# Moving the expert and combine stages of a fused conv, attention and expert kernel in its schedule

## The reference

```python
x = x + conv3x3(group_norm(x, 32 groups), W0)            # 64 -> 64 channels, pad 1
t = tokens(x)                                            # (8, 3136, 64)
a = layer_norm(t)
q, k, v = a @ Wq.T + bq, a @ Wk.T + bk, a @ Wv.T + bv
t = t + softmax(q @ k.T / 8) @ v                         # over all 3136 tokens of an image
y = layer_norm(t)
gates = top 2 of softmax(y @ gate_w + gate_b), normalised to sum 1     # 16 experts
t = t + sum over the 2 experts e of gate_e * ((silu(y @ w1[e]) * (y @ w2[e])) @ w3[e])
```

## Time and profile before

| | |
|---|---|
| median of 3 runs | 3304.51 us |
| profiled execution | 3304.37 us, its span 3301.5 us |
| PE busy | 2755.8 us (83%) |
| DVE, ACT, POOL busy | 1950.5, 1426.9, 1004.9 us |
| granted PE clock | 0.92 of full speed on average |
| last score matmul of the attention | starts at 2899.9 us |
| last slice of the experts copied | 3194.6 us |

### The profile page before, as it was taken

How to read it: one execution, slowest core, us unless ns; L and a number is a source line. 1 busy time by engine, 2 the same in 40 slices (tenths; PEclk the granted TensorE clock), 3 DMA queues, 4 the chain that set the end, 5 groups by cost and what they waited for, 6 DMA issues and landing times.

```text
span 3301.5 us, 47374 instructions
## 1 busy us (share of the span) xinstructions
PE 2755.8 (83%) x14345; PEld 1688.3 (51%) x14345; DVE 1950.5 (59%) x5316; ACT 1426.9 (43%) x3169; POOL 1004.9 (30%) x1084
## 2 busy tenths in 40 slices
PE   0489998998999999998999899998999898967760
PEld 0245554554555555555555455554555555545550
DVE  1366667667666666668566765667656656442221
ACT  0134444444555544554445454454544454523330
POOL 4000002221212134234242332423324323347444
PEclk9679999999999999999999999999999999965555
DMA  6200000111111111211112111111111111123321
GB/s 142 63 21 20 19 16 26 30 29 33 47 43 41 44 44 50 54 44 52 51 50 52 49 49 51 50 49 40 50 47 41 38 43 43 42 64 91 82 60 31
DMA packets 218415, 156.13 MB, mean 47 GB/s; under 512 B 94400, under 2 KB 208832, under 8 KB 218176
## 3 DMA queue, kind: packets, MB, share of 16 engines
q1 hardware_dynamic: 187008, 106.12, 12.2%
q0 software_dynamic: 31168, 46.98, 5.9%
HBM read 89.29 MB, written 63.70 MB: 46 GB/s over the span
## 4 chain that ended last, share of the span: by engine, by line
PE 58%; DVE 24%; issue 8%; POOL 6%; ACT 2%; DMA 2%; SPq 1%; POOLq 0%; DVEq 0%; ACTq 0%
PE ps_o L1060 17%; DVE max_part L788 9%; PE ps_s L1047 8%; PE ps_m L1026 8%; PE ps_s L1049 6%; PE ps_x L1202 5%; PE ps_z L1085 4%; POOL got L515 3%; PE ps_x L1217 2%; PE ps_z L1210 1%; POOL sorted_x L502 1%; PE ps_y L1136 1%; PE ps_y L1120 1%; DVE top_i L845 1%; DVE got L944 1%
## 5 line engine op out<-in xcount | busy, mean ns | idle before, releaser
L788 DVE TENSOR_REDUCE max_part<-ps_m 112x1 f32<-112x448 f32 x1568 | 947.9, 621 | 528.5 <-PE ps_m L1026 518.9
L636 ACT ACTIVATE prob<-ps_s 112x448 f32<-112x448 f32 x1568 | 848.9, 543 | 598.8 <-PE ps_s L1049 575.1
L1026 PE MATMUL ps_m<-k_a,q_a 128*112 128x448 f32 x1568 | 589.3, 394 | 140.4 <-DVE max_part L788 129.5
L1060 PE MATMUL ps_o<-prob,v_s 112*64 112x448 f32 x3136 | 695.9, 566 | 0.3 <-issue 0.3
L1047 PE MATMUL ps_s<-q_a,k_a 128*112 128x448 f32 x1568 | 661.9, 422 | 16.0 <-ACT prob L636 9.9
L1049 PE MATMUL ps_s<-q_b,k_a 128*112 128x448 f32 x1568 | 573.5, 366 | 0.0
L502 POOL DMA_INDIRECT sorted_x<-xn,slot x448 | 427.3, 954 | 283.7 <-issue 260.3
L515 POOL DMA_INDIRECT got<-sorted_y,slot x448 | 424.9, 948 | 213.8 <-issue 126.5
L1026 PEld LDWEIGHTS ps_m<-k_a,q_a 128*112 128x112 f32 x1568 | 276.4, 176 | 311.1 <-DVE max_part L788 273.1
L525 POOL TENSOR_TENSOR ln_s<-ln_s,minus_half 112x4 f32<-112x4 f32 x56 | 58.1, 1037 | 1175.7 <-DVE ln_s L706 1175.7
L1047 PEld LDWEIGHTS ps_s<-q_a,k_a 128*112 128x112 f32 x1568 | 276.2, 176 | 184.5 <-issue 123.4
(11 more groups left out here) (170 smaller groups left out, 3004.0 us busy)
## 6 DMA issues: line engine op xcount, KB each, us to landing
fx<-sorted_x SPq DMA_DIRECT2D x48, 384.0 KB
sorted_y<-fy SPq DMA_DIRECT2D x48, 320.0 KB, 3.1
fx<-sorted_x SPq DMA_DIRECT2D x56, 256.0 KB
xh<-in_x SPq DMA_DIRECT2D x96, 126.0 KB, 2.7
x_st<-in_x SPq DMA_DIRECT2D x100, 112.0 KB, 2.6
sorted_x<-fy POOLq DMA_DIRECT2D x24, 320.0 KB
sorted_x<-xn,slot POOLq DMA_INDIRECT x448
got<-sorted_y,slot POOLq DMA_INDIRECT x448
```

Source lines behind the costliest of these rows:

```text
L636: a.activation(prob[(at.n * TILES + i) % PROBS][:], ps_s[i % 2][0:TILE, 0:CHUNK], ACT.Exp).then_inc(s["p_ready"], 1)
L788: v.tensor_reduce(max_part[:, m % PER, m // PER:m // PER + 1], ps_m[m % 2][0:TILE, 0:CHUNK], AX.X, ALU.max).then_inc(s["max_red"], 1)
L1026: t.matmul(ps_m[m % 2][0:TILE, 0:CHUNK], q_a[:, bass.ds(n % 2, 1), j * TILE:(j + 1) * TILE].rearrange("p a c -> p (a c)"), k_a[u % 2][:, k ...
L1060: t.matmul(ps_o[side:side + CHANNELS, 0:CHUNK], v_s[u % 2][:, i, :], prob[(n * TILES + i) % PROBS][:], start=(i < 2), stop=(i >= TILES - 2 ...
```

## The change

- **Experts** follow 11 bodies behind the attention instead of 15 (`LAG["experts"] = CHUNKS + 4`). Their slices of an image then fall on the bodies with c = 4, 5, 6, 0, 1, 2, 3, and no longer on c = 1 to 6 and 0. The short slice of 2 pairs was in c = 0 beside the routing; it is now in c = 3.
- **Scatter**: the seven scatters of an image, one in each body before, are done in three bodies: one at the end of c = 0 (after the routing), three in c = 1, three in c = 2. In c = 1 and c = 2 the first of them is ahead of norm2 and norm1, the rest behind norm1. In bodies 57 and 58, where there is no attention, all three are first. Consecutive scatters count on two semaphores.
- **Combine**: images 0 to 5 are combined in four bodies: two chunks in c = 5, two in c = 6, two in c = 0, one in c = 1. Of two chunks in a body the first has DVE at step 11, PE and ACT at step 12; the second has steps 19 and 21, as before. Images 6 and 7 are combined in bodies 61 to 74, one in each, at steps 22 and 23. Gather buffers and `tc` are doubled: a gather waits for the combine before the last, and it is issued in the body before its combine.
- **Experts without attention**: body by body, all pairs go through one pipeline that doesn't stop at body ends: at step 1 + 4 * place PE has fx of pair k, hidden of k-1, down of k-3, turn of k-2. "hidden" alternates between the two score banks `ps_s`. `fy` is doubled. SP stores a slice one body later, behind the loads of the slice after next and behind the body's output store.

```diff
-LAG = {"pre": -CHUNKS, "post": 1, "scatter": 1 + CHUNKS, "experts": 1 + 2 * CHUNKS, "combine": 1 + 3 * CHUNKS}
+LAG = {"pre": -CHUNKS, "post": 1, "experts": CHUNKS + 4}
+SCATTERS = ((0,), (1, 2, 3), (4, 5, 6), (), (), (), ())
+COMBINES = {5: (0, 1), 6: (2, 3), 7: (4, 5), 8: (6,)}
+COMBINE_AT, COMBINED_AT = (11, 19, 22), (12, 21, 23)
+LATE = ALL + 5
+LAST = LATE + 2 * CHUNKS - 1
...
+    def combines(self):
+        if self.n >= LATE:
+            return [(2, ALL - 2 * CHUNKS + self.n - LATE)] if self.n <= LAST else []
+        image, place = (self.u - 3, self.c + CHUNKS) if self.c < 2 else (self.u - 2, self.c)
+        chunks = COMBINES[place] if place in COMBINES and 0 <= image < BATCHES - 2 else ()
+        return [(slot + 2 - len(chunks), CHUNKS * image + c) for slot, c in enumerate(chunks)]
+
+    def stores(self):
+        if self.attends:
+            return [self] if self.active("experts") else []
+        ends = self.n == ALL + LAG["experts"] - 1
+        return [At(*divmod(n, CHUNKS)) for n in range(self.n - 1, self.n + ends) if ALL <= n < ALL + LAG["experts"]]
...
+def expert_steps(at):
+    if at.attends:
+        return [(i, name, at, pair) for i, _, name, pair in EXPERT_STEPS
+                if at.active("experts") and pair < at.pair_count()]
+    steps, pairs = [], alone_pairs()
+    here = [k for k, (mine, _) in enumerate(pairs) if mine.n == at.n]
+    if here and here[-1] == len(pairs) - 1:
+        here += [len(pairs) + k for k in range(3)]
+    for place, k in enumerate(here):
+        for name, behind in (("fx", 0), ("hidden", 1), ("gated", 1), ("down", 3), ("turn", 2)):
+            if 0 <= k - behind < len(pairs):
+                steps.append((1 + 4 * place, name) + pairs[k - behind])
+    return steps
...
             def body(at):        # SP
-                if at.active("combine"):
-                    k = at.index("combine")
-                    wait_apart(sp, s["c_ready"], ONE + k)
+                for _, k in at.combines():
+                    if k >= 1:
+                        wait_apart(sp, s["c_ready"], ONE + k - 1)
...
                 load_slice(at, 0)
-                if at.active("combine") and at.attends:
-                    store_out(at)
+                for place, k in at.combines():
+                    if place == 0:
+                        store_out(k)
                 load_slice(at, 1)
-                if at.active("combine") and not at.attends:
-                    store_out(at)
+                for place, k in at.combines():
+                    if place:
+                        store_out(k)
...
-            def gather(at):
+            def gather(k):
...
-                wait_apart(pool, s["c_ready"], ONE + k)
+                if k >= 1:
+                    wait_apart(pool, s["c_ready"], ONE + k - 1)
...
             def body(at):        # POOL
-                for stage, name in (("scatter", scatter), ("post", norm2), ("pre", norm1), ("combine", gather)):
-                    if at.active(stage):
-                        name(at)
+                early = at.scatters() if at.c else []
+                early = early[:1] if at.attends else early
+                for m in early:
+                    scatter(m)
+                if at.active("post"):
+                    norm2(at)
+                if at.active("pre"):
+                    norm1(at)
+                for _, k in At(*divmod(at.n + 1, CHUNKS)).combines():
+                    gather(k)
+                for m in at.scatters()[len(early):]:
+                    scatter(m)
...
             def body(at):        # PE; ACT and DVE alike
+                    for place, k in at.combines():
+                        if i == COMBINED_AT[place]:
+                            combined(k)
+                    for step, name, mine, pair in experts:
+                        if step == i:
+                            expert(mine, name, pair)
```

More of the change, by code:

```diff
@@ L106, in index @@
     def index(self, stage):
[L108 to L114, removed]
+        return min(max(self.n - LAG[stage], 0), ALL)
     def active(self, stage):
@@ L418, in _ @@
[L418 to L427, removed]
-                body(five, (u + 1, CHUNKS - 1))
-                body(At(u, CHUNKS - 1), (u + 2, 0) if u + 2 < BATCHES else None)
+                for place, k in at.combines():
+                    if place:
+                        store_out(k)
@@ L430, in _ @@
+            for n in range(-CHUNKS - 1, LAST + 1):
+                at, nxt = [At(*divmod(m, CHUNKS)) for m in (n, n + 1)]
+                body(at, (nxt.u + 1, nxt.c) if n >= -CHUNKS and nxt.u + 1 < BATCHES else None)
             sp.wait_ge(s["stored"], ONE + 16 * ALL)
@@ L499, in scatter @@
                     wait_apart(pool, s["fx_b_in"], ONE + (b - 1) * (CHUNKS - 1) * 16)
-                for j in range(at.chunk("scatter") * PER, (at.chunk("scatter") + 1) * PER):
+                for j in range(c * PER, (c + 1) * PER):
                     for k in range(TOP):
@@ L644, in body @@
                             events[name](at)
-                    for step, _, name, pair in (EXPERT_STEPS if at.attends else EXPERT_STEPS_ALONE):
-                        if step == i and at.active("experts") and pair < at.pair_count():
-                            expert(at, name, pair)
+                    for place, k in at.combines():
[4 more added lines that the diff above has]
+                            expert(mine, name, pair)
                     if i == NEXT_QUERIES and at.ahead:
@@ L968, in body @@
                             events[name](at)
-                    for step, _, name, pair in (EXPERT_STEPS if at.attends else EXPERT_STEPS_ALONE):
-                        if step == i and at.active("experts") and pair < at.pair_count():
-                            expert(at, name, pair)
+                    for place, k in at.combines():
+                        if i == COMBINE_AT[place]:
+                            combine(k)
+                    for step, name, mine, pair in experts:
+                        if step == i:
+                            expert(mine, name, pair)
                     if i == 3 and at.u == -1:
@@ L1195, in expert @@
                             for j in range(2 * (last - first)):
[L1196 removed]
+                                picked[2 * (f - pair + first) + j] = (code >> (j * DIGIT)) & (EXPERTS - 1)
                 elif name == "hidden":
[L1198 removed]
+                    (bank_x if at.attends else bank_h[f % 2]).take(("hid_ready", f + 1))
                     pe.wait_ge(s["fxT_ready"], ONE + f + 1)
```

179 lines of the change are left out of this document (91 added, 88 removed).

## The result

The changed kernel takes 3299.3 us (median of 17 runs, 3295.9 to 3304.0), the kernel before 3304.5 (17 runs, 3299.9 to 3310.1): ratio 0.9984, interval 0.9977 to 0.9991. That is 5 us faster where 13.5 were forecast. Its profiled span is 3295.9 us.

A forecast was written before the change was run, and what follows sets the result against it. PE bounds 56 bodies, then latencies and POOL's DMAs set a 401.6 us tail. Terms: -103 + 26.5 - 5 + 62 + 6 = -13.5, from 3304.4 to 3291 us; own range 3275 to 3306, 8 in 10 3243 to 3327.

The forecast's parts named there:

- part 3: Combines under the attention: 17 early ones at 4.9 us each, 83 + 40 - 61 = +62 us.
- rival A: Early combines under attention cost 7 us each, the clock down behind the wait: 36 us more, 3327; chance 0.20.
- The group norm's power behind a gather: POOL's order in c = 6: the power comes some 1.6 us late, DVE and PE wait, 4 bodies, +6 us.
- Routing beside pairs: Routing bodies get 3 more pairs, c = 3 loses 3; PE's idle time swallows part: -5 us for 6 bodies.
- 26.5: Under the attention: 17 more pairs at 1.56 us each, +26.5 us.
- The late combine's 1.8: In attention bodies, a combine at steps 19 and 21 costs 1.8 us.
- the pair's 1.56: In attention bodies, an expert pair costs 1.56 us beside the attention.
- The tail: From the last scores to the span's end: 299 us against 401.6, a loss of 103 us.
- Rival B: Early combines under attention cost no more than late ones: 53 us less, 3238; chance 0.15.
- C: Tail: the pipeline keeps PE full at the upper clock, a place at 1.9 us, total 3273; chance 0.18.
- D: c = 0 and 1: late slots put norm2 behind two scatters, 3 us in 7 bodies, 21 in all, 3312; chance 0.05.
- E: Tail: PE stays at the lower clock, a place takes 2.8 us, 10 us more, 3301; chance 0.10.

The follow-up runs named there:

- p_after: The changed kernel with each indirect DMA replaced by a plain one of the same size to and from fixed rows: 3229.8 us.
- p_early9: The changed kernel with plain DMAs in place of indirect ones and the early combine's sum at step 9 instead of 11 on DVE: 3117.8 us.
- The filler: The changed kernel with plain DMAs and twenty useless products on PE ahead of the early combine's wait: 3203.2 us; with its own DMAs, ratios 1.0104 to 1.018.
- early9: The changed kernel, own DMAs, with the early combine's sum at step 9 instead of 11 on DVE: 3190.8 us, ratio 0.9655 to the kernel before.
- first three groups: Follow-up runs of variants of the changed kernel, measured group by group; the kernel before took 3866, 3868 and 3933 us there.
- last two groups: Follow-up runs with plain DMAs, then variants of the changed kernel with their own DMAs; the kernel before took 3305.8 and 3303.8 us.
- second group: The unedited changed kernel as a control, rerun beside three of its variants: ratio 1.0167 to the kernel before at 3868.0 us.
- spread: The changed kernel with one combine a body, at steps 19 and 21, for images 0 to 4: ratios 1.0156 and 1.0171 to the kernel before.

## Why the prediction was wrong

The direction was right, the size was not: -5 us instead of -13.5. That the time still lies in the forecast's own range (3275 to 3306), and the attention and the tail within the bounds set for them, is luck in part: terms that came out cheaper hid two thirds of what the wrong one cost.

- **The failed step is the size of the early combine in part 3** ("I take 4.9"). It measured 6.3 us each: steps 11 to 15 of the 17 bodies are 107 us longer in all than in the kernel before (5.9, 6.7 and 6.65 in bodies 33, 34 and 35). In c = 0 a part of that belongs to the added pairs: body 14, which has them and no combine, grew 0.8 in these steps. The difference in attention between p_after and p_early9 says 6.3 too. 17 x 1.4 = 24 us missing, which is rival A's mechanism short of its full 7. The wait was as worked out: 3.94 to 4.17 us in sixteen of the bodies against 4.1, and 2.42 in body 55. Body 33 adds up as 3.95 (wait) + 0.98 (transposes) + 0.42 (the down, slower) + 1.63 (step 13) - 0.97 (given back in steps 14 and 15) = 6.0, against 5.9 measured. At the upper clock the transposes would take 0.56, and the down and step 13 nothing more: the clock is 2.5 of it and the rest 3.5, where I had 1.0 and 3.9. I had priced a fall at 1.5 us, which is what the values alone lose in the earlier trace rows, and averaged it down to 1.0, since it might not come each time. It came every time, and all products behind the wait pay, not the values alone. The filler gave back 1.3 of it in these steps; its products run 1.4 us past the end of the wait, which is about what is missing. The granted clock fell behind each of the 17 waits (0.63 to 0.84 over steps 12 and 13). By the Trainium skill ("TensorE: Matmul & The Clock Gate", Why this matters for your kernels) each of the 17 was to pay; the trace agrees.
- **The group norm's power behind a gather** (+6) cost nothing: steps 24 to 27 of c = 6 take 0.75, 2.42, 0.81 and 0.91 us before and after. The body got longer by the early combine, so POOL had the time. The cover came from the cost beside it: in early9, without that cost, the term is there, some 1.5 us in each of the four bodies. The mechanism was right, and the sum had left out that the two terms are not independent.
- **Routing beside pairs** (-5) was worth somewhat more, and by another way. The six bodies with c = 0 grew 60.7 us, of which 33.8 lie in steps 11 to 15 of the five with an early combine: 27 us for 18 pairs instead of 28, so routing swallowed next to nothing (2.5 to 7.6 us for three pairs, by body). c = 3 fell from 50.8 to 43.1, 5.9 for three pairs beyond the combine's 1.8: the first two pairs of a body cost 1.0 each there, the next three 2.0. In all about -8.5. With the terms in place the sum is 26.5 + (107 + 40 - 61) - 8.5 = 104, measured 97.7. Of the 6 left some may be counted twice in c = 0, as said; the rest was not taken apart.
- **The late combine's 1.8 and the pair's 1.56** held roughly: 49.1 without, 50.6 with one combine (c = 1), so 1.5 to 1.7; and five pairs 7.9 us, 1.6 each on average.
- **The tail** came out at 298.3 us where 299 was forecast, with slots at +36.5 (38), scatters from +37.7 to +107.5 (to 108) and the first of the last gathers at +218.0 (219). Within it a place took 2.25 us, not 2.5, and a combine between pairs some 4 us, not 2.5: two errors that cancelled. The runs give 29 of the 103 us to the second hidden bank and 22 to the gathers that no longer wait just before them; the rest was not taken apart.
- **Rival B** (early as cheap as late) was false at step 11, and at step 9 even too dear. **C** was half right: the clock was 0.82 instead of 0.53, but a place did not reach 1.9. **D**: norm2 ran on time, 11.3 us into c = 1 as before. **E** gives 3301, near the measured 3299, by a mechanism that the trace denies: PE did not stay at the lower level, with four transposes in every pair. One bank more moved the clock from 0.52 to 0.82 with the same instructions in each pair, so the transposes alone did not hold it down. What did was not told apart: PE is busy 69.5 of 90 us in the one row and 68.0 in the other, but runs 298 operations in the one and 383 in the other. The rule of the Trainium skill ("TensorE: Matmul & The Clock Gate", Part 4: PE-mode transpose) did not decide here.

## What to carry to other kernels

In an engine's fixed order a consumer must stand behind the point where its producer can be done, read for both engines from one timeline: two steps on DVE's side were worth 3.3% of the changed kernel, where the whole change had been worth 0.16%. Count a wait of a few us on PE with what the lower clock costs behind it, each time. Look for an idle stretch behind the new work: here the combine was free where one followed, once it didn't wait. And terms of a sum can cover each other: the late power on POOL cost nothing while PE waited, and 6 us once it didn't.

## What was not expected

- **Stops beside GpSimd's DMAs.** In the first three groups all engines stood still while POOL issued indirect DMAs; the changed kernel shows nothing of the kind in its own profile above, nor do the runs of the last two groups. Body 15 (c = 1) of the changed kernel in the second group: PE's hidden products run at 943.7 to 944.3, the tanh that needs them starts at 959.5, and POOL issues every 1.24 us through all of it.

```profile
942.84 0.54 ACT L677 ACTIVATE prob<-ps_s 112x448 f32<-112x448 f32 x1
959.49 0.38 ACT L644 ACTIVATE th<-ps_x 128x256 f32<-128x256 f32 x1 [16.12 <-remote]
```
```profile
956.38 0.94 POOL L532 DMA_INDIRECT sorted_x<-xn,slot  x1 [0.30 <-issue]
957.61 0.93 POOL L532 DMA_INDIRECT sorted_x<-xn,slot  x1 [0.30 <-issue]
958.85 0.93 POOL L532 DMA_INDIRECT sorted_x<-xn,slot  x1 [0.30 <-issue]
```

  The longer the unbroken row of issues, the longer the stop: with one gather behind norm1, step 15 took 6.2 us instead of 2.4 (spread), and the body with three scatters 80 us instead of 50.6. The bodies with packed scatters grow most (c = 1, from 50.6 to 80), which fits that the changed kernel was 1.7% slower than before there and 0.16% faster here; the kernel before has no profile with stops beside which to show it. One chip showed both conditions in different groups. What brings it about stays open.
- **A plain DMA is cheaper to issue.** POOL spends 0.53 us on one, 0.93 to 0.94 on an indirect one with 0.30 between. The last gathers of p_after are 6.9 us apart instead of 10, and wait again for a combine, 2.7 us each; its tail is 231 us instead of 298.
